# Cross-attention kernel: values of the older item behind the first half unit, and row sums of items 32 and 33 with fewer things ahead of them

## The reference

```python
x = x + attention(ln1(x) -> q, k, v; mask) @ w_ao           # A: self attention
x = x + attention(ln2(x) -> q; enc -> k, v; mask) @ w_co     # B: cross attention
x = x + gelu(ln3(x) @ w1 + b1) @ w2 + b2                     # C: MLP, 512 -> 2048 -> 512
a = layer_norm(enc)                                          # D: gated cross attention
Q, K, V = x @ Wq.T, a @ Wk.T, a @ Wv.T
attn = softmax(where(mask, Q @ K.T * HEAD_DIM ** -0.5, -inf))
x = x + tanh(gate) * ((attn @ V) @ Wo.T)
```

## Time and profile before

| | us |
|---|---|
| median of 3 runs | 1098.52 |
| lowest and highest | 1095.3, 1100.08 |
| the profiled execution | 1095.96 |
| its span, first to last instruction | 1094.2 |
| TensorE busy | 1066.9 |
| VectorE busy | 821.1 |
| ScalarE busy | 703.8 |
| GpSimd busy | 482.2 |

### The profile page before, as it was taken

The page is one execution under the profiler, slowest core; times in us unless marked ns, Lnnn a source line. Parts: engine busy times, 40 slices in busy tenths (PEclk is TensorE's granted clock), DMA queues, the critical chain, the costliest instruction groups (busy, mean ns, idle before and its releaser), DMA issues.

```text
span 1094.2 us, 24221 instructions
## 1 busy us (share of the span) xinstructions
PE 1066.9 (98%) x8741; PEld 924.9 (85%) x8741; DVE 821.1 (75%) x1299; ACT 703.8 (64%) x2354; POOL 482.2 (44%) x361
## 2 busy tenths in 40 slices
PE   7989999999999999999999999999999999999998
PEld 6888888888888888887898888888888988888886
DVE  6678887778888788888867667768697466666767
ACT  4687777777888878787444444444455276666676
POOL 3665666657767766767513122113032222222310
DMA  6366666577777777564243151341647646666621
GB/s 217 98 194 202 204 186 194 175 221 214 213 236 227 202 226 235 169 189 147 87 145 106 58 173 58 116 146 47 213 134 261 221 131 203 208 200 206 203 72 60
DMA packets 145831, 185.92 MB, mean 170 GB/s; under 512 B 17856, under 2 KB 88752, under 8 KB 145712
## 3 DMA queue, kind: packets, MB, share of 16 engines
q1 hardware_dynamic: 145712, 184.37, 54.0%
HBM read 122.59 MB, written 61.73 MB: 168 GB/s over the span
## 4 chain that ended last, share of the span: by engine, by line
PE 45%; DVE 16%; ACT 12%; POOL 7%; issue 6%; DMA 6%; SPq 3%; DVEq 0%; ACTq 0%; POOLq 0%
PE psum L1087 15%; PE psum L1068 14%; POOL prob L2202 7%; PE psum L890 7%; ACT prob L1372 4%; ACT prob_blocks L1372 3%; DVE prob L1752 3%; PE psum L882 3%; PE psum L1007 3%; DVE ln_tile L1687 3%; DMA ln_tile<-stream 3%; DVE negmax L1765 3%; DMA normalised<-ln_tile 2%; ACT second_prob_blocks L1372 2%; ACT inputs_transposed L1410 2%
## 5 line engine op out<-in xcount | busy, mean ns | idle before, releaser
L890 PE MATMUL psum<-inputs_hi,weights_hi 128*128 128x256 f32 x768 | 223.6, 291 | 5.4 <-POOL inputs_lo L2188 2.3
L890 PE MATMUL psum<-inputs_lo,weights_hi 128*128 128x256 f32 x768 | 217.0, 283 | 0.0
L890 PE MATMUL psum<-inputs_hi,weights_lo 128*128 128x256 f32 x768 | 216.9, 282 | 0.0
L2202 POOL TENSOR_TENSOR prob<-prob,mask_bias 128x1024 f32<-128x1024 f32 x64 | 152.7, 2408 | 98.5 <-DVE prob L1752 96.4
L890 PEld LDWEIGHTS psum<-inputs_hi,weights_hi 128*128 128x128 f32 x768 | 146.7, 191 | 10.8 <-issue 4.9
L1765 DVE TENSOR_REDUCE negmax<-prob 128x8 f32<-128x1024 f32 x96 | 115.6, 1211 | 50.1 <-POOL prob L2202 50.0
L1372 ACT ACTIVATE prob<-prob,negmax 128x128 f32<-128x128 f32 x384 | 148.2, 390 | 0.1
L890 PEld LDWEIGHTS psum<-inputs_lo,weights_hi 128*128 128x128 f32 x768 | 147.0, 191 | 0.2
L890 PEld LDWEIGHTS psum<-inputs_hi,weights_lo 128*128 128x128 f32 x768 | 146.9, 191 | 0.0
L2188 POOL TENSOR_TENSOR inputs_lo<-inputs_transposed,inputs_hi 128x512 fp32r<-128x512 f32 x70 | 93.3, 1354 | 93.1 <-DVE inputs_hi L1725 60.9
L1372 ACT ACTIVATE prob_blocks<-prob,negmax 128x128 f32<-128x128 f32 x304 | 117.5, 389 | 25.5 <-DVE negmax L1765 25.3
(11 more groups left out here) (132 smaller groups left out, 2654.3 us busy)
## 6 DMA issues: line engine op xcount, KB each, us to landing
prob_turned<-prob_blocks SPq DMA_DIRECT2D x38, 512.0 KB, 3.0
prob<-prob_turned SPq DMA_DIRECT2D x152, 128.0 KB, 3.5
weights_whole<-weights_in SPq DMA_DIRECT2D x72, 256.0 KB, 3.2
inputs_transposed<-normalised SPq DMA_DIRECT2D x120, 128.0 KB, 2.8
normalised<-ln_tile SPq DMA_DIRECT2D x24, 512.0 KB, 2.8
context<-row_sums_spread SPq DMA_DIRECT2D x188, 64.0 KB, 2.1
stream<-residual SPq DMA_DIRECT2D x42, 256.0 KB, 3.1
ln_tile<-stream SPq DMA_DIRECT2D x32, 256.0 KB, 3.9
```

Source lines behind the costliest of these rows:

```text
L890: mm = pe.matmul(ps[:, bank, GT * part:GT * part + GT], w[:, slot, c, o], a[:, buf, c, :], start=c == 0 and i == 0, stop=c == KC - 1 and i ...
L2202: pool.tensor_tensor(half, half, mb.unsqueeze(1).to_broadcast([128, 8, T]), ALU.add).then_inc(s_biased, 1)
```

## The change

Three things. In steps 35 to 44 (g - 2 in `WHOLE`), `times_v(g - 2)` is no longer first: it stands behind `scores(g)` and the first half unit, ahead of `row_sums(g - 1)`. Item 32 writes its values into one bank like the `WHOLE` ones, so `context(32)` waits for all four groups of products, and `row_sums(33)` waits for `probs_out(32)`, which empties `T_BANK + 1`, and no longer for `context(32)`. In `first_steps_of_d`, `exps(33, 0)` moves behind `half_out(D, 1, 4)` and `row_sums_out(32)`.

```diff
         def value_bank(g, half):
-            return T_BANK if g in WHOLE else T_BANK + half
+            return T_BANK if g in WHOLE or g == 32 else T_BANK + half
...
                     if g - 1 in WHOLE:
                         pe.wait_ge(s_rc, g)
                     else:
-                        pe.wait_ge(s_cx, 2 * g)
+                        pe.wait_ge(s_pta, copied_by_act(g - 1, 1))
...
-                if st.ends:
+                if st.ends and g - 2 not in WHOLE:
                     times_v(g - 2)
                 if g:
                     scores(g)
...
                 project(*st.units[0], U_BANK, (0, 1) if g else (1,))
+                if g - 2 in WHOLE:
+                    times_v(g - 2)
                 if late:
...
                 exps(32, 3)
                 half_out(D, 1, 3)
-                exps(33, 0)
                 half_out(D, 1, 4)
                 row_sums_out(32)
+                exps(33, 0)
                 probs_out(32)
...
-                dve.wait_ge(s_pv, 4 * g + (4 if g in WHOLE else 2 * h + 2))
+                dve.wait_ge(s_pv, 4 * g + (4 if value_bank(g, 1) == T_BANK else 2 * h + 2))
```

## The result

The changed kernel takes 1106.71 us (median of 6 runs, 1103.55 to 1108.1) where the kernel before takes 1096.43 (median of 6, 1095.3 to 1100.08). The ratio is 1.0078, 95% interval 1.0064 to 1.0093: slower, by 8.6 us (7.0 to 10.2) by that ratio, while the two medians lie 10.3 apart. Forecast was 5.9 us slower.

A forecast was written before the change was run, and what follows sets the result against it. It took a ring of ScalarE and VectorE, not TensorE, as the bound: 3.8 us from even steps less 0.5 made 3.3, step 44 brought 5.9; on the median 1098.52 that gave 1104.4 us, range 1099 to 1109, at widest 1097 to 1110.

The forecast's parts named there:

- double step: Time for two steps between 896 and 1023 us: 28.1 us by VectorE's reciprocals, TensorE's own work 27.4; forecast to become 29.0.
- Part 1: Edits in step 33 to items 32 and 33: TensorE 1.4 us ahead, the ring and what follows at most 0.5 earlier.
- the ring: ScalarE's exponentials and VectorE's maxima waiting for each other, never for TensorE, 896 to 1023 us; 28.10 us per two steps.
- Part 2, even steps: Moved times_v, steps 36 to 42: q copy to context 5.35 us against 4.40, adding 0.95 to the ring each, 3.8 together.
- Odd steps: Moved times_v in odd steps: v copy to context 4.13 us against 4.40, nothing added, 0.2 to 0.3 left.
- Step 44: Late context(42) holds up the reciprocal of item 43; row_sums(43) 5.9 us late, the ring 3.3 late in step 43.
- To the end: Behind row_sums(43) TensorE runs almost without a gap on dependent work, so 5.9 us go through to the end.
- the bound of 0.5%: 5.5 us of the whole time, about what can be told from no change; the forecast was 0.54%.
- slower by more: Outcome of the whole kernel slower by more than 0.5%; chance 0.50, against same 0.44 and faster by more 0.06.
- R1: Rival: TensorE is the bound and its idle time goes, 4.8 us gained, 1093.7 us; chance 0.10.
- R2: Rival: the 0.95 us delay is paid once, later even steps run as before, step 44 3.0 late, 1101.5 us; chance 0.10.
- R3: Rival: odd steps run over too, up to 0.3 us in each of five, 1106 us; chance 0.10.

The follow-up runs named there:

- e8: Kernel before, order untouched, VectorE's block transpose of the inputs in even steps 34 to 44 cut from 1024 columns to 64, results wrong; ratio 0.9969.
- e3: Changed kernel with times_v first in all steps as before, keeping the edits to items 32 and 33; ratio 1.0000.
- e11: The changed kernel unaltered, timed and profiled again; ratio 1.0070 to the kernel before.
- e2: Changed kernel with the move of times_v kept in odd steps only (35 to 43); ratio 0.9991 to the kernel before.
- e5: Changed kernel with times_v(42) put back to the head of step 44, steps 35 to 43 still moved; ratio 1.0034 to the kernel before.
- e6: Changed kernel, but in step 44 VectorE takes the reciprocal of item 43 ahead of context(42); ratio 1.0044 to the kernel before.
- e1: Changed kernel with the move of times_v kept in even steps only (36 to 44); ratio 1.0045 to the kernel before.
- e4: Kernel before with only the move of times_v in steps 35 to 44, steps 32 to 34 as before; ratio 1.0067.
- e7: Changed kernel, but in steps 34 to 43 ScalarE copies the third half unit ahead of exps(g, 1); ratio 1.0043 to the kernel before.
- e9: Changed kernel with times_v(g - 2) directly behind scores(g), ahead of the first half unit, in steps 35 to 44; ratio 1.0001 to the kernel before.

## Why the prediction was right, point by point

**What bounds.** Right, and e8 shows it by itself: 4.1 us gained by taking 1.0 us from VectorE in every second step. TensorE's own double step was put at 27.4; e8 has 27.33 where TensorE bounds.

**Part 1.** The forecast was 0.5 us for the ring and the end, 1.4 for TensorE. Measured 0.5 (e3); the reciprocal of item 33 comes 897.49 - 882.13 = 15.36 us after `scores(33)`, where 896.25 - 880.43 = 15.82 was before; and `row_sums(33)` 898.48 - 882.13 = 16.35 us after `scores(33)` against 898.39 - 880.43 = 17.96, 1.6 earlier.

**Part 2, even steps.** The mechanism was right in its place, sign and parity. The term of 0.95 us per even step was a little too small: 29.16 - 28.09 = 1.07, and 1.03 in e11. The path from the q copy to `context` was priced well: 5.37 - 4.40 = 0.97. Most of what was missing lies behind it, from `context` to the next reciprocal: 941.81 - 927.88 = 13.93 us in the changed kernel, and in the kernel before 13.87 (from 925.63 to the row below). The forecast let this stretch move as it was. Four times 1.07 is 4.3, less 0.5 leaves 3.8: the reciprocal of item 42 comes (1029.28 - 882.13) - (1023.76 - 880.43) = 3.8 us late, forecast 3.3.

```profile
939.50 0.26 DVE L1773 RECIPROCAL rtotal<-total 128x16 f32<-128x16 f32 x1 [1.69 <-ACT second_prob_blocks L1372]
```

**Odd steps.** Nothing added, as said (e2), though TensorE waits 1.39 us there for the v copy; the odd step had that room.

**Step 44.** From 3.8 to 6.3, forecast from 3.3 to 5.9: 2.5 and 2.6. e5 and e6 give both halves of the reason, the late values and the place of the reciprocal.

**To the end.** 6.4 us in the trace, forecast 5.9: the sum of the same steps, short by 0.5 in the even steps. The forecast also took TensorE's new wait of 2.9 us to cost its own length only. In e11 and e1 a stretch of low clock followed it and cost 1.3 to 1.5 us more, which no term had. Whether that makes up the rest of the timed 8.6 us is not shown.

**What was luck.** 1106.71 lies in the stated range, but the forecast of 1104.4 stood on a median of three runs, 1098.52. On the median of six, 1096.43, the same 5.9 us give 1102.3. And 5.9 us was so near the bound of 0.5% that "slower by more" had a chance of only 0.50. The trace's 6.4 us are 0.58%, over that bound, but not by much.

**The rivals.** R1 (TensorE is the bound) fell with e2, e8 and the result. R2 (paid once) fell with four waits of 0.9 us. R3 (odd steps run over) fell with e2. The Trainium skill, "Perfetto Trace Analysis", says in the section Identifying the Most-Contended Engine to improve the busiest engine first, and in the section Optimization Strategy to look at its gaps and make what they wait for start sooner or finish faster. The change did only half of that: it moved the waiting product back instead of its data forward. The gaps ahead of `times_v` were closed to nothing and the time rose, so in this case gaps of the busiest engine were no measure of what could be gained.

## What to carry to other kernels

Before closing a gap of the busiest engine, look whether another chain of engines returns in a constant period: if its releasers never name the busy engine, the gap may be slack, as here, and moving a producer on the busy engine behind other work lengthens that chain by whatever it exceeds the old path. Price a moved instruction at its reader: here the path from copy to context, 5.4 us against 4.4, gave the loss per step and the step in which nothing was lost. And look at the one step where the pattern ends, since there the lists of the other engines have another order; half of the loss lay in step 44 alone.

## What the runs showed of the hardware

TensorE idled for 2.85 to 2.86 us in step 44 of five traces (changed, e1, e4, e7, e11). In e11 and e1 the clock then went for a while to the lower of its two levels (granted 0.5, that is 1.2 of 2.4 GHz; mean 0.57 from 1044 to 1048 us and 0.59 from 1047 to 1051). It fell within the wait in e11 and 1.3 us behind its end in e1. The work behind took 1.3 to 1.5 us more. In e7 the same wait came with a longer stretch:

```profile
1041.00:1048.00 7.00, 6.02 (x29) 6.02 (x30) 5.44 (x8) 0.74 (x2) 0.60 (x1) 0.51 0.46 144
```

and from `row_sums(43)` to the end took 57.5 us instead of 55.0. In the first trace of the changed kernel and in e4 the same wait was followed by none. So it is not certain in each execution, three of five here; what decides it is left open. The eight traces without that wait have no low stretch behind `scores(33)`.

The same pair of events stands near 505 us, in steps that no edit touches. There TensorE waits for a reciprocal, 1.2 us in six traces and 2.2 to 2.3 us in seven, and a low stretch begins late in the wait or up to 1.1 us behind its end in four of the seven (e2, e5, e7, e9) and in none of the six. From e9, whose granted clock is 0.50 from 507 to 509 us:

```profile
506.56 0.38 PE L947 MATMUL psum<-identity,rtotal 128*16 128x128 f32 x1 [2.30 <-DVE rtotal L1775]
```

That the idle time causes the low clock is argued from what stands ahead of it in these traces; no run varied the length of a wait alone.
